# A fused attention block and deformable convolution: the offset convolution in three slots and the deform matmul in two

## The reference

```python
om = conv3x3(offset_feat, w_offmask) + b_offmask            # 216 channels
val = bilinear samples of feat_up at (y + ky + dy, x + kx + dx), times sigmoid(mask)
feat_align = relu(einsum('bgckhw,ogck->bohw', val, w_dcn) + b_dcn)
```

## Time and profile before

| | us |
|---|---|
| median of three runs (13206.21 to 13208.47) | 13208.17 |
| the profiled execution | 13224.19 |
| its span, first to last instruction | 13222.4 |
| PE busy | 10509.4 |
| ACT busy | 8994.9 |
| DVE busy | 7803.0 |
| POOL busy | 6817.1 |
| mean granted TensorE clock | 0.922 |

### The profile page before, as it was taken

One profiled execution on the slowest core, in us unless ns is written; L12 is line 12 of the kernel. 1 busy time (PEld: TensorE's weight loads), 2 busy tenths in 40 slices (PEclk: granted clock), 3 DMA queues, 4 the chain that ended last, 5 costly groups with the idle time before them and its releaser, 6 DMA issues.

```text
span 13222.4 us, 500910 instructions
## 1 busy us (share of the span) xinstructions
PE 10509.4 (79%) x187900; PEld 7906.7 (60%) x187900; DVE 7803.0 (59%) x11602; ACT 8994.9 (68%) x19604; POOL 6817.1 (52%) x6194
## 2 busy tenths in 40 slices
PE   3678888888888888888888888888888888841888
PEld 2346666666666666666666666666666666631667
DVE  6456656565665656566565656666565666621654
ACT  1357777777777777777777777777777777731777
POOL 0034554545455454645455464545545454566467
PEclk7789999999999999999999999999999999975999
DMA  4234454544445454544445454444544444431454
GB/s 130 57 88 121 116 124 117 122 118 119 123 117 122 119 122 115 123 121 120 119 119 125 111 125 121 121 119 122 122 118 119 119 121 121 118 68 30 117 128 121
DMA packets 1846525, 1512.65 MB, mean 114 GB/s; under 512 B 1006689, under 2 KB 1381985, under 8 KB 1841569
## 3 DMA queue, kind: packets, MB, share of 16 engines
q1 hardware_dynamic: 1834468, 1474.31, 45.2%
q0 software_dynamic: 9216, 2.38, 0.2%
HBM read 1297.68 MB, written 178.25 MB: 112 GB/s over the span
## 4 chain that ended last, share of the span: by engine, by line
PE 41%; issue 17%; ACT 10%; DVE 8%; POOLq 7%; DVEq 6%; POOL 4%; SPq 3%; DMA 2%; ACTq 1%
PE bank_small L998 8%; PE windows L1040 8%; PE bank_small L1051 5%; POOLq L696 4%; PE bank_scores L917 4%; PE windows L1014 3%; PE bank_post L971 3%; DVE bank_post L1541 3%; POOLq L698 2%; DVEq L1540 2%; DVEq L1526 2%; POOL gbuf L772 2%; ACT hats L1249 2%; ACT hats L1253 2%; DVE prod L1597 1%
## 5 line engine op out<-in xcount | busy, mean ns | idle before, releaser
L1597 DVE TENSOR_TENSOR prod<-windows,wy 128x640 f32<-128x640 f32 x4032 | 3295.4, 821 | 3113.4 <-PE windows L1014 2169.2
L695 POOL TENSOR_TENSOR prod<-prod 128x768 f32<-128x768 f32 x1344 | 2457.5, 1828 | 4561.6 <-DVE prod L1597 4558.7
L1040 PEld LDWEIGHTS windows<-fx,hats 64*64 64x64 f32 x129024 | 2615.0, 136 | 1538.0 <-issue 1452.0
L1040 PE MATMUL windows<-fx,hats 64*64 64x80 f32 x129024 | 3259.6, 240 | 325.9 <-ACT valt L1296 126.2
L1249 ACT ACTIVATE hats<-hats,cst 128x512 f32<-128x512 f32 x4032 | 2886.9, 716 | 119.3 <-DMA hats<-sample_columns 62.9
L1253 ACT ACTIVATE hats<-hats 128x512 f32<-128x512 f32 x4032 | 2523.4, 626 | 0.5
L1541 DVE SCALAR_TENSOR_TENSOR bank_post<-xpad,lepw,bank_post 128x448 f32<-128x448 f32 x2688 | 1851.9, 689 | 222.4 <-issue 1.3
L697 POOL TENSOR_TENSOR prod<-prod 128x384 f32<-128x384 f32 x1344 | 1530.5, 1139 | 197.2 <-issue 7.8
L998 PE MATMUL bank_small<-wom,ofp 128*128 128x216 f32 x8064 | 1616.0, 356 | 0.0
L700 POOL TENSOR_TENSOR val<-prod 128x384 f32<-128x384 f32 x1344 | 1401.5, 1043 | 268.4 <-issue 230.2
L998 PEld LDWEIGHTS bank_small<-wom,ofp 128*128 128x128 f32 x8064 | 1493.9, 196 | 30.3 <-issue 1.5
(11 more groups left out here) (196 smaller groups left out, 12930.6 us busy)
## 6 DMA issues: line engine op xcount, KB each, us to landing
hats<-sample_columns SPq DMA_DIRECT2D x2688, 336.0 KB
ksel<-k_windows SPq DMA_DIRECT2D x3136, 32.0 KB
vsel<-v_windows SPq DMA_DIRECT2D x3136, 32.0 KB
fx<-map_columns SPq DMA_DIRECT2D x64, 420.0 KB
xpad<-in_x SPq DMA_DIRECT2D x17, 1568.0 KB, 11.2
q_windows<-qb SPq DMA_DIRECT2D x112, 224.0 KB, 2.8
k_windows<-kb SPq DMA_DIRECT2D x112, 224.0 KB, 3.6
v_windows<-vb SPq DMA_DIRECT2D x112, 224.0 KB, 3.2
```

Source lines behind the costliest of these rows:

```text
L695: pool.tensor_tensor(v[:, :, 0:n], v[:, :, 0:n], v[:, :, n:2 * n], ALU.add)
L1040: last[h] = pe.matmul(o[m], hat[:, m], fx[XP * h:XP * h + XP, g, row:row + WR, :].rearrange("p r c -> p (r c)"), start=True, stop=True)
L1597: dve.tensor_tensor(o, x, w.unsqueeze(3).to_broadcast([128, 2, CP * WR, CG]), ALU.mult).then_inc(s_wm, 1)
```

## The change

Only PE's and ACT's programs are edited. PE's `offsets` gets a part: part 0 (taps 0 to 2, with all the waits) is issued in slot 7 of tile t for tile t+3, part 1 (taps 3 to 5) in slot 8 for tile t+3, part 2 (taps 6 to 8, and the signal) in slot 0 for tile t+2, which is the same tile counted from the next one. PE's `deform` gets a part: taps 0 to 4 in slot 5, taps 5 to 8 and the signal in slot 6; the first part waits for three of the five copies of samples, the second for all. ACT's ReLU moves from slot 5 to slot 6. The last two tiles of the last image run both parts one after the other.

```diff
--- before.py
+++ after.py
@@ -988,15 +988,18 @@
                     pe.matmul(bp[:, 0:BAND], woff[:, 0, :], t1[:], start=True, stop=False)
                     pe.matmul(bp[:, 0:BAND], woff[:, 1, :], ub[b % 2], start=False, stop=True).then_inc(s_p6, 1)
 
-            def offsets(i, t):
-                pe.wait_ge(s_of, cnt(i, NB, min((2 * t + 2) // WS, NB - 1) + 1))
-
-                wait(pe, s_fl, cnt(i, NT, t))
-                wait(pe, s_rt, cnt(i, NT, t - 4))
-                for k in range(KK):
+            def offsets(i, t, part):
+
+                if part == 0:
+                    pe.wait_ge(s_of, cnt(i, NB, min((2 * t + 2) // WS, NB - 1) + 1))
+
+                    wait(pe, s_fl, cnt(i, NT, t))
+                    wait(pe, s_rt, cnt(i, NT, t - 4))
+                for k in range(3 * part, 3 * part + 3):
                     at = conv_rows(t)(k)
                     mm = pe.matmul(bm[:, 0:3 * S], ofp[:, at:at + TP], wom[:, k, :], start=(k == 0), stop=(k == KK - 1))
-                mm.then_inc(s_om, 1)
+                if part == 2:
+                    mm.then_inc(s_om, 1)
 
             def turn_columns(i, t):
                 pe.wait_ge(s_pxy, cnt(i, NT, t + 1))
@@ -1043,13 +1046,17 @@
                 for h in range(2):
                     last[h].then_inc(s_win, 1)
 
-            def deform(i, t):
-                pe.wait_ge(s_ve, cnt(i, NP * NT, NP * t + NP))
-                wait(pe, s_rt, cnt(i, NT, t))
-                pe.wait_ge(s_fl, upto(i, t + 5))
-                for k in range(KK):
+            def deform(i, t, part):
+
+                ks = (range(5), range(5, KK))[part]
+                pe.wait_ge(s_ve, cnt(i, NP * NT, NP * t + (3, NP)[part]))
+                if part == 0:
+                    wait(pe, s_rt, cnt(i, NT, t))
+                    pe.wait_ge(s_fl, upto(i, t + 5))
+                for k in ks:
                     mm = pe.matmul(bm[:, 216:344], wdcn[:, k, :], valt[t % 2][:, k, :], start=(k == 0), stop=(k == KK - 1))
-                mm.then_inc(s_do, 1)
+                if part == 1:
+                    mm.then_inc(s_do, 1)
 
             def x_first(i, n):
                 w = step_of(n, 4)
@@ -1082,6 +1089,7 @@
             def body(xi, di):
                 for t in range(NT):
                     fi, ft = tile_of(di, xi, t + 2)
+                    gi, gt = tile_of(di, xi, t + 3)
                     pi, pt_ = before(di, t, 2)
                     for q in range(Q):
                         n = t * Q + q
@@ -1093,13 +1101,15 @@
                         if xi is not None:
                             x_first(xi, n)
                         if fi is not None and q == OM:
-                            offsets(fi, ft)
+                            offsets(fi, ft, 2)
+                        if gi is not None and q >= Q - 2:
+                            offsets(gi, gt, q - Q + 2)
                         if fi is not None and q == PXT:
                             turn_columns(fi, ft)
                         if fi is not None and q == PXT + 1:
                             sum_outside(fi, ft)
-                        if pi is not None and q == WD:
-                            deform(pi, pt_)
+                        if pi is not None and q in (WD, WD + 1):
+                            deform(pi, pt_, q - WD)
                         if xi is not None:
                             x_rest(xi, n)
 
@@ -1115,7 +1125,8 @@
                 pe.wait_ge(s_ve, (NIMG * NT + t - NT) * NP + p)
                 turn_samples(NIMG - 1, t, p, hb[p % 2])
                 if p == NP - 1:
-                    deform(NIMG - 1, t)
+                    for part in range(2):
+                        deform(NIMG - 1, t, part)
 
         @block.scalar
         def _(act):
@@ -1339,7 +1350,7 @@
                             row_sizes(ni, nt)
                         if fi is not None and q == PXT + 1:
                             masks(fi, ft, 0)
-                        if pi is not None and q == WD:
+                        if pi is not None and q == WD + 1:
                             relu(pi, pt_)
                         if ni is not None and q == WYH:
                             row_hats(ni, nt)
```

## The result

| | before | changed |
|---|---|---|
| median of four runs each, us | 13207.2 (13199.1 to 13208.5) | 12990.0 (12973.0 to 12998.9) |
| span of the profiled execution, us | 13222.4 | 12982.3 |

The ratio is 0.9844, 95% interval 0.9829 to 0.9858: faster by 217 us, where 543 were forecast. The direction held and the time lies within the range, but only two fifths of the forecast gain came. In the profiled executions it is 240 us. Later runs are compared through their ratio to the kernel before, which took 13180 to 13207 us beside them.

A forecast was written before the change was run, and what follows sets the result against it. No engine is full; PE and DVE wait for each other, with PE at most two slots ahead. 33.5 us a double pass times 15 (503) plus 40 in the last pass gave 543 saved: 12665 us, range 12420 to 13010.

The forecast's parts named there:

- the quiet tile: One attention tile of 26.74 us, forecast to lose 1.6 us, down to DVE's floor of 25.1 us.
- Nine plain attention tiles at 2.0 ... 18: Attention tiles of a double pass, bounds 1.6 and 4.8 us each; taken at 2.0, 18 us a pass saved.
- part 2: Offset convolution split over slots 7, 8 and 0: 0.9 us saved, PE's 8.1 to 9.1 us covered by DVE's 8.18 and PE's lead.
- GELU blocks: Seven tiles a pass: GELU in slot 6 +4 each, slot 3 +1.5 each, slot 0 -1.5 each; 6.5 us saved.
- qkv: Six qkv tiles, where PE has 13.0 us idle in all: between 0 and 13, taken as 5 us a pass saved.
- Last tiles: Last tiles of a double pass (122.9 us, PE 103.4): between 0 and 19.5, taken as 4 us saved.
- Last pass: Deformable-only pass of 463.0 us: at most 55 won before POOL is the bound, taken as 40 us saved.
- rival C: Spread-out PE work lowers TensorE's granted clock; at 0.78 attention tiles take 27.8 us, 13460 us in all; chance 0.06.
- The later ReLU and part 0's wait: ReLU in slot 6 and part 0's wait for an earlier tile's ReLU: forecast to cost nothing unless ACT is late.
- A: Little lands: waits belong to a chain through ACT and attention steps and only shift; about 12980 us; chance 0.13.
- signs given for a right forecast: Listed trace signs, such as offset add's wait under 8 us, weighting waits about 120, plain tile 25.1 to 25.4, POOL's under 20.
- D: No change: gains in plain tiles are eaten by GELU blocks, each losing 3 to 4 us; chance 0.03.

## Why the prediction was right or wrong

**What bounds the kernel.** Right: waits between PE and DVE at two slots; PE nearly the bound in qkv; DVE's floor in the quiet tile, 25.1 worked out and 24.95 found. Wrong: that this floor is what bounds the other plain tiles.

**How far off.** The sum per pass was 33.5 and 14.5 came. Of the 19.0 missing, 17.8 are one term, the plain tiles.

**The term that failed: "Nine plain attention tiles at 2.0 ... 18".** Measured: 0.2. Only four of the nine (13, 15, 20, 22) have lepe taps on DVE through slots 6 to 8, and they gave 5.5, 1.4 each. Tiles 9, 11, 16 and 18 have steps of an MLP block in these slots; I had counted a block's tile as the one in which GELU lies. There 1.1 us were paid in slot 8, in tiles 11 and 18 as much again in slot 7, and the four lost 3.1 us a pass. Tile 8 lost 2.2. The quiet tile that was taken as the least of its kind was its best. The failed step is the overlap of part 2, "8.1 to 9.1 against 8.18 of DVE ... and PE's lead of up to two slots absorbs the rest": it was about right for a tile with lepe taps, whose three slots took 8.2 us before and 8.2 to 8.4 after, and it was applied to tiles where DVE has 3.8 us of work in the three slots (9 and 16) or 5.0 (11 and 18), and where PE was already busy 7.5 to 8.2 of 8.2 to 8.3 us. There the three slots took 1.8 to 3.1 us more, against 0.6 to 1.2 won in slot 5 and 0.3 to 1.3 in slot 0.

**GELU blocks, 6.5 forecast:** 8.5 measured. Slot 6: 4 each forecast, 2.8 in the tile itself. Slot 0: -1.5 each forecast, -0.9 with its clock loss, and more with the slots of tiles 9, 16 and 23. Slot 3: +1.5 each forecast, 2.8 measured, paid for in tiles 11 and 18.

**qkv, 5 forecast:** 4.1, of which tiles 1 and 6 gave 3.4; tiles 2, 4 and 5 gave nothing at all: -2.2 and -0.9 in slots 0 and 5, +0.9, +1.0 and +1.0 in slots 6 to 8.

**Last tiles, 4 forecast:** 23 lost 1.7, 25 to 27 won 2.1, 0 and 7 won 1.3: 1.7 in all.

**Last pass, 40 forecast:** 21. The tile time that the forecast comes to was reached where the clock stayed up, in part of the tiles; of the time over 15.53 us a tile 14 us lie in tiles with low clock and 10 in tiles without. So rival C's mechanism had a share in this pass. In the passes with both halves it cost little: the attention stage shown has 0.94 before and after, and PE's time at the lower level rose from 79 to 87 us a pass (from 6.7 to 15.6 in tiles 10, 17 and 24, from 8.5 to 1.0 in 14 and 21), which costs at most half of the 8 us more, an estimate.

**The waits.** The later ReLU and part 0's wait cost nothing in plain tiles, as forecast. In tile 8 ReLU stands behind a late DMA on ACT, and PE idled 3.3 us on average before part 0; it idled 3.6 us there before the change too, in front of the turn of the probabilities.

**The rivals.** The time is that of A (12980 forecast), but not by A's reason: with the deform matmul alone the 217 us were already there, and the convolution added gains and losses of equal size. Of the signs given for a right forecast these came: the offset add's wait gone, ReLU's wait down by more than half, output matmuls of slot 6 at 2.5, those of slot 0 up, PE's busy time the same. These did not: weighting waits at 120 (175.5 came); a plain tile at 25.1 to 25.4 (tile 15 alone, by its mean; the others are at 25.8 to 32.4 us by theirs); the last pass from 463 to about 425 (441.8 for the same 27 tiles); and POOL's wait in the last pass under 20:

```profile
POOL prod L695 <- DVE prod L1608: 39.8, 28, 3.7
```

it is 39.8 (54.9 before, for a stretch one tile shorter). Of the signs of D, longer GELU tiles, tiles 10, 17 and 24 showed it, 12, 14, 19 and 21 the opposite.

## What to carry to other kernels

Spreading a burst pays where the engine behind it is the slower one over the slots that take the pieces, and costs one for one where the bursting engine is itself late; so classify each stretch by what the *receiving* slots hold, slot by slot, and not by what the giving slot holds. Look at every long wait near the edit for what lies under it now: work under another engine's long instruction cost nothing here and kept the clock up, and taking it away cost twice, at its new place and by the clock. If the split has several parts, time each alone: here one of them carried the whole gain.

## What the runs showed of the hardware

A hole of 1.69 us before the output matmuls never came with a fall of the granted clock (28 of 28 at 2.52 us), holes of 2.1 to 2.7 us did in 24 of 42 cases (up to 4.8 us for the same six passes), and holes of 3.6 to 3.8 us in all. The hole alone does not tell it: behind twelve idle matmuls and a hole of 0.94 us the fall came in 5 of 14. The fall can come once in every tile of a steady loop: 17.07 us a tile with 3.41 us at the lower level each time, against 15.5 us at full clock. A kernel with more matmuls in the holes ran that pass in 448.7 us where the other took 472.7, one trace each. I had expected the evening out to leave the clock alone in the last pass.
